# Shared experts' down products moved to the joining phase, with a chunked last batch and early first gathers

## The chip, the cores and the metric

One core of a Trainium2 chip runs the whole program. Its engines are TensorE (PE; PEld is its weight load), VectorE (DVE), ScalarE (ACT) and GpSimd (POOL); SyncE (SP) issues most of the DMAs, ACT and POOL issue some. They run their own instruction lists and meet by semaphores. The metric is the time of one execution on the device in microseconds (us).

## What is computed

A stack of four residual steps on 4 x 512 tokens of width 512. Each step is x = x + layernorm(f(layernorm(x))). The first f is a state-space layer, the second a mixture of experts, the third a gated delta-rule attention, the fourth an expert layer with routing by batch. The change touches the end of the first, the whole of the second, and the begin of the third. The second, cut to what matters:

```python
scores = softmax(x @ gate_weight.T)
topk_w, topk_idx = top_k(scores, 2)
gu = einsum('th,efh->tef', x, gate_up_weights)        # 8 experts, F = 352
act = silu(gu[..., :F]) * gu[..., F:]
y = einsum('tef,te,ehf->th', act, combine, down_weights)
sgu = x @ shared_gate_up.T                            # shared experts, 2 x 352
sact = silu(sgu[:, :Fs]) * sgu[:, Fs:]
y = y + sact @ shared_down.T
```

## The kernel before

Everything is float32 and runs in phases. A phase ends when all engines, SP too, are through with their lists, so also with the stores that SP waits for. A batch is 512 tokens (NB = 4 of them), handled as TPB = 4 chunks of 128 tokens on the partitions, or turned (features on the partitions) in XT, a tile of 4 batches x 4 x 512 that lasts through the phases.

**State space** (`phase_ssm`). Its last part norms the result y of each batch, adds it to x, norms the new x into yn, stores x and yn to HBM (x1 and xn), and PE turns yn into XT, ACT copying out of PSUM. For each of the last two batches DVE does it step by step for all four chunks: `y_mean`, `y_rstd` (the reciprocal root by 15 small DVE instructions), `y_apply`, `x_mean`, `x_rstd`, `x_apply`. PE turns the last batch at `turn(NB + 3)`.

**Shared experts and routing** (`phase_moe_shared`). For each batch PE makes five pairs of products g and u (`up`; the sixth pair, the one that carries the routing logits, is made for all batches first), ACT takes silu(g), DVE multiplies by u into `act`; then `downs(b)` makes 24 products of 128 x 512 into four PSUM banks, ACT copies them to `y` (`copies`), SP stores them to HBM (`y_shared`). Beside this DVE works out which slot each token takes, and POOL scatters the token numbers to HBM and reads them back (`rt.token`); SP loads the routed experts' gate and up weights.

**Routed experts** (`phase_moe_experts`). 40 tiles of 128 slots. SP first issues the loads of eight experts' down weights (`w_dn`, 768 KB each). POOL gathers a tile's rows from xn by token number (`gather`), two buffers deep; the first gather is its first work in the phase. PE turns the rows, makes g and u, turns the next tile's rows, and makes the down product of the tile before (`down`). In tile 0, which has no tile before it, PE waits at that place for all of `w_dn` (`dn_loaded`).

**Joining phase** (`phase_moe_out`). For each batch POOL gathers the two routed results of every token (`picked`, 8 gathers of 256 KB), SP loads y_shared and x1 of the batch, DVE sums them (`sums`), then DVE and ACT in turns do the two norms and the residual (`scale_y`, `residual`, `scale_x`), PE turns the result and ACT copies it to XT (`take_turned`). In between PE makes 12 units of the next layer's projections in three PSUM banks `pj` (`unit`), and ACT and DVE their convolution taps. After it comes the delta phase.

The order on each engine is the order of the code; there is no scheduler. The place on which PE waits in the routed phase:

```python
                if is_first(t):
                    e.wait_ge(dn_loaded, 16 * NE)
                else:
                    down(t - 1, 1 - par)
                e.wait_ge(act_done, t + 3)
```

## Time and profile before

| | us |
|---|---|
| median of 3 runs (lowest, highest) | 3064.32 (3063.19, 3068.24) |
| the profiled execution | 3064.84 |
| its span, first to last instruction | 3063.1 |
| mean granted TensorE clock | 0.961 |
| PE busy | 2827.2 (92%) |
| DVE busy | 1840.4 (60%) |
| ACT busy | 1203.1 (39%) |
| POOL busy | 612.7 (20%) |
| state space, until | 439.2 |
| shared experts and routing, until | 696.7 |
| routed experts, until | 1041.7 |
| joining phase, until | 1174.6 |

Times in a row are us from the span's start, unless marked ns. In brackets stands how long the engine was idle before, and what ended it: "<-DMA x" a landed transfer, "<-issue" nothing that the profile shows. A matmul of float32 is two passes on PE and counts as x2. The granted clock is a share of 2.4 GHz, so 0.50 is 1.2 GHz.

### The profile page before, as it was taken

How to read it: one execution, taken by the hardware profiler on the slowest of the kernel's cores; microseconds unless marked ns; L12 is line 12 of the kernel's file. 1: busy time of each engine (PE TensorE's matmuls, PEld its weight loads, DVE VectorE, ACT ScalarE, POOL GpSimd, SP SyncE). 2: the span in 40 equal slices, each digit the busy share in tenths (PEclk: the TensorE clock that was granted, in tenths of full speed). 3: DMA queues.
4: the chain of work that ended last, by engine and by line, in shares of the span. 5: the costliest groups of instructions: out<-in, count | busy, mean ns of one | idle time of the engine just before them, and what ended most of it. 6: DMA issues, size and time to landing. Idle time of an engine off the chain costs nothing. (4 is left out here: it accounts for less than half of the span.)

```text
span 3063.1 us, 37789 instructions
## 1 busy us (share of the span) xinstructions
PE 2827.2 (92%) x13038; PEld 1586.5 (52%) x13039; DVE 1840.4 (60%) x4673; ACT 1203.1 (39%) x2198; POOL 612.7 (20%) x669
## 2 busy tenths in 40 slices
PE   7999979997999587899999999999999999999787
PEld 3444434444565344555566655666556665554232
DVE  5767742000111275777877778777787777637676
ACT  4545511001212144345544455444554455422232
POOL 1111201301111312033123331233312333110000
PEclk9999989998999888999999999999999999999899
DMA  3100142003221452011100111001110011227213
GB/s 124 47 14 28 42 172 102 14 14 144 65 65 63 174 217 101 1 43 61 65 28 29 42 62 64 28 29 43 63 63 28 29 42 59 80 82 245 76 45 97
DMA packets 78134, 213.64 MB, mean 70 GB/s; under 512 B 12032, under 2 KB 12944, under 8 KB 69392
## 3 DMA queue, kind: packets, MB, share of 16 engines
q1 hardware_dynamic: 58336, 166.31, 15.0%
q0 software_dynamic: 9264, 28.36, 2.9%
q10 hardware_dynamic: 10368, 16.83, 1.5%
q8 instruction: 96, 1.57, 0.2%
q14 instruction: 70, 0.57, 0.1%
HBM read 154.68 MB, written 56.79 MB: 69 GB/s over the span
## 5 line engine op out<-in xcount | busy, mean ns | idle before, releaser
L2137 DVE SCALAR_TENSOR_TENSOR c_conv<-c_ps_pj,c_conv_t,c_conv 128x511 f32<-128x511 f32 (+2 forms) x495 | 368.0, 746 | 85.6 <-ACT c_conv L1975 73.9
L1759 PE MATMUL c_ps_pj<-c_w_g,c_xs 128*128 128x512 f32 x512 | 227.7, 592 | 0.0
L1668 POOL TENSOR_SCALAR c_gate<-c_gate 128x512 f32<-128x512 f32 x64 | 40.8, 637 | 932.6 <-ACT c_gate L1967 932.6
L1742 PE MATMUL c_ps_pj<-c_xs,c_w_v 128*128 128x512 f32 x480 | 225.8, 593 | 0.0
L1742 PE MATMUL c_ps_pj<-c_xs,c_w_k 128*128 128x512 f32 x480 | 218.0, 597 | 6.0 <-DMA c_xs<-xt_d 6.0
L1742 PE MATMUL c_ps_pj<-c_xs,c_w_q 128*128 128x512 f32 x360 | 195.3, 677 | 0.3
L1975 ACT ACTIVATE c_conv<-c_ps_pj,c_conv_t 128x512 f32<-128x512 f32 x165 | 127.9, 775 | 87.9 <-PE c_ps_pj L1742 85.8
L1098 DVE TENSOR_TENSOR x_act<-x_hs,x_ps_u 128x352 f32<-128x352 f32 x40 | 20.9, 521 | 228.0 <-ACT x_hs L1083 228.0
L2156 DVE TENSOR_TENSOR c_block_X<-c_block_X,c_block_t 128x126 f32<-128x126 f32 (+22 forms) x496 | 142.6, 288 | 17.0
L2152 DVE TENSOR_TENSOR c_block_t<-c_block_L,c_block_X 128x126 f32<-128x126 f32 (+22 forms) x496 | 139.4, 281 | 17.0
L1759 PEld LDWEIGHTS c_ps_pj<-c_w_g,c_xs 128*128 128x128 f32 x512 | 93.6, 190 | 100.0 <-issue 100.0
L880 DVE TENSOR_TENSOR b_act<-b_hs,b_ps_u 128x512 f32<-128x512 f32 (+1 forms) x24 | 16.5, 686 | 209.9 <-PE b_ps_u L802 209.9
L2027 ACT ACTIVATE c_err<-c_negL 32x128 f32<-32x128 f32 x256 | 78.6, 307 | 151.1 <-DVE c_negL L2221 146.4
L1742 PEld LDWEIGHTS c_ps_pj<-c_xs,c_w_k 128*128 128x128 f32 x480 | 87.3, 192 | 93.5 <-issue 87.2
L277 PE MATMUL a_ps_gt<-XT,a_w_gate 128*128 128x512 f32 x256 | 120.0, 613 | 6.5 <-ACT a_th L386 6.5
L1049 PE MATMUL x_ps_g<-b_w_gu,x_xT 128*128 x320 | 123.3, 467 | 1.6 <-issue 0.8
L245 POOL TENSOR_SCALAR a_skip<-a_xc,a_col_d 128x512 f32<-128x512 f32 x32 | 62.1, 1940 | 300.4 <-ACT a_xc L394 168.6
L1050 PE MATMUL x_ps_u<-b_w_gu,x_xT 128*128 x320 | 122.0, 463 | 0.0
L268 PE MATMUL a_ps_pj<-XT,a_w_in 128*128 128x512 f32 x256 | 119.1, 609 | 0.8 <-ACT XT L370 0.8
L294 PE MATMUL a_ps_yo<-a_w_out,a_th 128*128 128x512 f32 x256 | 115.7, 600 | 0.0
L1809 PE MATMUL c_ps_kk<-c_kT 128*128 128x128 f32 x512 | 101.5, 280 | 12.5 <-DVE XT L2223 7.0
L2086 ACT ACTIVATE c_err<-c_ps_z 128x512 f32<-128x512 f32 x64 | 38.2, 597 | 190.1 <-PE c_ps_z L1927 188.5
(499 smaller groups left out, 5907.2 us busy)
## 6 DMA issues: line engine op xcount, KB each, us to landing
c_G<-cum_d SPq DMA_DIRECT2D x16, 1024.0 KB, 4.7
c_xs<-xt_d SPq DMA_DIRECT2D x16, 1024.0 KB, 4.9
ot_d<-c_oT ACTq DMA_DIRECT2D x64, 256.0 KB, 2.0
b_w_gu<-in_w_gu SPq DMA_DIRECT2D x8, 1408.0 KB, 20.7
y_slots<-x_y SPq DMA_DIRECT2D x40, 256.0 KB, 2.0
a_x<-in_x SPq DMA_DIRECT2D x8, 1024.0 KB, 6.4
d_x<-x SPq DMA_DIRECT2D x32, 256.0 KB, 2.9
d_switch<-in_switch_w SPq DMA_DIRECT2D x4, 2048.0 KB, 15.3
```

Of the source, the lines that this page charges most:

```text
L268: mm = e.matmul(pj[c % 2][:, :], w_in[:, k, c * P:(c + 1) * P], XT[:, b, k, :], start=(k == 0), stop=(k == KD - 1))
L277: mm = e.matmul(gt[:, :], w_gate[:, k, c * P:(c + 1) * P], XT[:, b, k, :], start=(k == 0), stop=(k == KD - 1))
L294: mm = e.matmul(yo[t % 2][:, :], th[:, b % 2, c, t * P:(t + 1) * P], w_out[:, c, :], start=(c == 0), stop=(c == CT - 1))
L1049: e.matmul(g_ps[par][:, 0:FE], xT[par][:, k, :], w_gu[:, expert, k, 0:FE], start=(k == 0), stop=(k == KD - 1))
L1050: mm = e.matmul(u_ps[par][:, 0:FE], xT[par][:, k, :], w_gu[:, expert, k, FE:2 * FE], start=(k == 0), stop=(k == KD - 1))
L1742: mm = e.matmul(bank_of[xb][u][:, :], w["kqv"[u // HG]][:, k, (u % HG) * DH:(u % HG + 1) * DH], xs[xb][:, k, :], start=(k == 0), stop=(k = ...
L1759: mm = e.matmul(pj[(xb + i) % 2][:, :], xs[xb][:, k, i * P:(i + 1) * P], w["g"][:, k, :], start=(k == 0), stop=(k == KD - 1))
L1809: e.matmul(kk[:, h, :], chunk(kT, h, c), chunk(kT, h, c), start=True, stop=True)
L1975: e.activation(conv[:, u % 4, :], bank_of[buf][u][:, :], ACT.Identity, bias=conv_t[buf][:, m, h, TAPS:TAPS + 1], scale=conv_t[buf][:, m, h ...
L2137: e.scalar_tensor_tensor(oc, bank_of[buf][u][:, 0:SEQ - s], conv_t[buf][:, m, h, TAPS - 1 - s:TAPS - s], oc, ALU.mult, ALU.add).then_inc(c ...
L2152: e.tensor_tensor(t, block_L[:, i + 1:BB, i].unsqueeze(2).to_broadcast([P, n, k]), block_X[:, i, 0:k].unsqueeze(1).to_broadcast([P, n, k]) ...
L2156: e.tensor_tensor(below, below, t, ALU.add).then_inc(sub_step, 1)
```

## The change

1. **Chunks.** The last batch of the state-space phase is normed chunk by chunk: DVE makes mean and variance of one chunk, ACT the reciprocal root (logarithm, exponential with scale -0.5), DVE goes on with the next chunk's work meanwhile. Batch 2 keeps the old form.
2. **Downs kept.** Batches 2 and 3 (`KEPT`) have no down products, copies and stores in the shared phase. Their activations stay: five tiles of each in XT, which is free there, the sixth in the space of `s_gu0`, where DVE copies it. The shared down weights are loaded again in the routed phase, two DMAs of 768 KB behind the eight of `w_dn` on SP, into the last six tiles of XT. The joining phase makes the eight products (6 matmuls each): seven first of all on PE, the eighth after the first batch is turned. ACT copies each out of `pj` into one of four buffers and issues its store itself: five in front of its first norm, one each after `scale_y(0)`, `scale_x(0)` and `take_turned(0)`. The first unit waits for the last copy.
3. **Gathers.** The gathers of tiles 0 and 1 are issued by POOL at the end of the shared phase, right behind the token table's load. Its loop in the routed phase starts with tile 2 and waits for a copy of its own from two tiles earlier, not for the one just made.
4. **Wait.** The wait for `w_dn` moves from tile 0 into `down`, so to the first down product.

The core of the diff:

```diff
+GATED = len(FT) - 1
+UNGATED = [f for f in range(NSH * len(FT)) if f != GATED]
+KEPT = [NB - 2, NB - 1]
...
+            def root(v, c):
+                at = ve if v == 0 else rt
+                e.wait_ge(last_mean[v], c + 1)
+                e.activation(at[:, c:c + 1], mv[:, c, 1:2], ACT.Ln, bias=con["eps"][:, :]).then_inc(last_ln[v], 1)
+                e.wait_ge(last_ln[v], c + 1)
+                e.activation(rs[:, c:c + 1], at[:, c:c + 1], ACT.Exp, scale=-0.5).then_inc(last_rstd[v], 1)
             take_y(NB - 1, 0)
             take_y(NB - 1, 1)
             turn_tile(NB + 2, 0)
+            root(0, 0)
+            root(0, 1)
             take_y(NB - 1, 2)
             turn_tile(NB + 2, 1)
+            root(1, 0)
+            root(0, 2)
             turn_tile(NB + 2, 2)
+            root(1, 1)
             take_y(NB - 1, 3)
             turn_tile(NB + 2, 3)
...
+            root(0, 3)
+            root(1, 2)
+            turn_tile(NB + 3, 0)
+            turn_tile(NB + 3, 1)
+            root(1, 3)
+            turn_tile(NB + 3, 2)
+            turn_tile(NB + 3, 3)
...
-            for b in range(NB - 2, NB):
-                y_mean(b)
-                y_rstd(b)
-                y_apply(b)
-                x_mean(b)
-                x_rstd(b)
-                x_apply(b)
...
+            def last_means(v, c):
+                e.bn_stats(st_[:, c, :], (y, x)[v][:, c, :]).then_inc(last_stats[v], 1)
+                e.wait_ge(last_stats[v], c + 1)
+                e.bn_aggr(mv[:, c, :], st_[:, c, :]).then_inc(last_mean[v], 1)
+            def last_means_y(c):
+                e.wait_ge(y_free, b * TPB + c + 1)
+                last_means(0, c)
...
+            def last_add(c):
+                e.wait_ge(last_rstd[0], c + 1)
+                e.wait_ge(turn_ready, TPB * (NB + b - 1) + c + 1)
+                e.tensor_scalar(yn[:, c, :], y[:, c, :], mv[:, c, 0:1], rs[:, c:c + 1], ALU.subtract, ALU.mult).then_inc(last_y, 1)
+                if c == 0:
+                    e.wait_ge(x_loaded, 16 * (NB + b + 1))
+                e.wait_ge(last_y, c + 1)
+                e.tensor_tensor(x[:, c, :], x[:, c, :], yn[:, c, :], ALU.add).then_inc(x_new, 1)
+                e.wait_ge(x_new, b * TPB + c + 1)
+                last_means(1, c)
...
+            def last_scale(c):
+                e.wait_ge(last_rstd[1], c + 1)
+                e.tensor_scalar(yn[:, c, :], x[:, c, :], mv[:, c, 0:1], rs[:, c:c + 1], ALU.subtract, ALU.mult).then_inc(x_normed, 1)
+            last_means_y(0)
+            last_means_y(1)
+            e.wait_ge(xn_stored, 16 * b)
+            last_add(0)
+            last_means_y(2)
+            last_add(1)
+            last_scale(0)
+            last_add(2)
+            last_scale(1)
+            last_means_y(3)
+            last_scale(2)
+            last_add(3)
+            last_scale(3)
...
+class KeptShared:
+    def __init__(self, XT, s_gu0):
+        tiles = XT[:, :, :, :].rearrange("p b k s -> p (b k) s")
+        self.w_dn = tiles[:, NB * KD - NSH * len(FT):, :].rearrange("p (i f) d -> p i f d", i=NSH)
+        gated = s_gu0[:, :, :].rearrange("p k f -> p (k f)")[:, 0:len(KEPT) * SEQ]
+        self.gated = gated.rearrange("p (b s) -> p b s", b=len(KEPT))
+        self.acts = tiles
+    def act(self, b, f):
+        j = KEPT.index(b)
+        if f == GATED:
+            return self.gated[:, j, :]
+        return self.acts[:, j * len(UNGATED) + UNGATED.index(f), :]
...
-            with e.Fori(0, NB) as b:
+            for b in range(NB - len(KEPT)):
                 for c in range(TPB):
                     e.wait_ge(y_copied, b * TPB + c + TPB + 1)
-                    stand(e, pr.waits_passed)
-                    e.dma_start(io["y_shared"][b].rearrange("(c p) d -> c p d", p=P)[c], y[c % 2][:, :]).then_inc(y_stored[c % 2], 16)
+                    e.dma_start(rows(io["y_shared"], b)[:, c, :], y[c % 2][:, :]).then_inc(y_stored[c % 2], 16)
...
+            e.wait_ge(token_loaded, 16)
+            for i in range(2):
+                e.tensor_copy(rows_in.one_token[i][:, :], rt.token[:, i:i + 1]).then_inc(first_copied, 1)
+            for i in range(2):
+                e.wait_ge(first_copied, i + 1)
+                e.indirect_dma_start(rows_in.x[i][:, :], None, io["xn"].rearrange("b s d -> (b s) d"),
+                                     bass.IndirectOffsetOnAxis(rows_in.one_token[i][:, :], 0)).then_inc(rows_in.loaded[i], 16)
...
-                downs(b)
+                if b not in KEPT:
+                    downs(b)
...
+                if b not in KEPT:
+                    copies(b)
...
+                    dst = kept.act(b, f) if b in KEPT and f != GATED else act[:, slot(b, f), :]
+                    e.tensor_tensor(dst[0:width, :], hs[s % 2][0:width, :], u_ps[s % 2][0:width, :], ALU.mult).then_inc(act_done, 1)
...
+                if b == NB - 1:
+                    acts(of_batch(b, 0, NF - 2))
+                    for k in KEPT:
+                        e.tensor_copy(kept.act(k, GATED)[0:GW, :], act[0:GW, slot(k, GATED), :]).then_inc(gated_kept, 1)
+                    acts(of_batch(b, NF - 2))
+                else:
+                    acts(of_batch(b))
...
+            for i in range(NSH):
+                e.dma_start(kept.w_dn[:, i], io["w_dn"][NE + i]).then_inc(kept_loaded, 16)
...
+                e.wait_ge(copied, t - 1)
...
-            tiles(e, gather)
+            with e.Fori(0, NS // 2 - 1) as p:
+                gather(p * 2 + 2, 0, p + 1)
+                gather(p * 2 + 3, 1, p + 1)
...
+                e.wait_ge(dn_loaded, 16 * NE)
...
-                if is_first(t):
-                    e.wait_ge(dn_loaded, 16 * NE)
-                else:
+                if not is_first(t):
...
+                    for stored in down_stored:
+                        e.wait_ge(stored, 16 * (b + 1))
...
+            def down(i):
+                b, c = downs[i]
+                if i >= PJ:
+                    e.wait_ge(down_copied, i - PJ + 1)
+                order = [GATED] + UNGATED
+                for f in order:
+                    width = FT[f % len(FT)][1]
+                    mm = e.matmul(pj[i % PJ][:, :], kept.act(b, f)[0:width, c * P:(c + 1) * P], kept.w_dn[0:width, f // len(FT), f % len(FT), :],
+                                  start=(f == order[0]), stop=(f == order[-1]))
+                mm.then_inc(down_ready, 1)
...
+                elif u == 0:
+                    e.wait_ge(down_copied, len(downs))
...
+            for i in range(len(downs) - 1):
+                down(i)
...
+                if b == 0:
+                    down(len(downs) - 1)
...
+            def take_down(i):
+                b, c = downs[i]
+                e.wait_ge(down_ready, i + 1)
+                if i >= STAGES:
+                    e.wait_ge(down_stored[i % STAGES], 16 * (i // STAGES))
+                e.activation(first.conv[:, i % STAGES, :], pj[i % PJ][:, :], ACT.Copy).then_inc(down_copied, 1)
+                e.wait_ge(down_copied, i + 1)
+                e.dma_start(rows(io["y_shared"], b)[:, c, :], first.conv[:, i % STAGES, :]).then_inc(down_stored[i % STAGES], 16)
...
+            for i in range(5):
+                take_down(i)
             scale_y(0)
+            take_down(5)
             scale_x(0)
+            take_down(6)
             take_turned(0)
+            take_down(7)
```

On DVE at the end of the state-space phase, before: the last batch from its y scale on; a_st, a_mv are statistics, a_ve, a_rt, a_rs the root's tiles.

```order
L512 TENSOR_SCALAR a_yn<-a_y,a_mv,a_rs 128x512 x4
L517 TENSOR_TENSOR a_x<-a_x,a_yn 128x512 x4
L480 BN_STATS a_st<-a_x 128x6 x4
L483 BN_AGGR a_mv<-a_st 128x2 x4
L114 TENSOR_SCALAR a_ve<-a_mv 128x4
L116 TENSOR_SCALAR a_rt<-a_ve 128x4
```

And now, from chunk 1's y scale on:

```order
L633 TENSOR_SCALAR a_yn<-a_y,a_mv,a_rs 128x512
L637 TENSOR_TENSOR a_x<-a_x,a_yn 128x512
L622 BN_STATS a_st<-a_x 128x6
L624 BN_AGGR a_mv<-a_st 128x2
L643 TENSOR_SCALAR a_yn<-a_x,a_mv,a_rs 128x512
L633 TENSOR_SCALAR a_yn<-a_y,a_mv,a_rs 128x512
L637 TENSOR_TENSOR a_x<-a_x,a_yn 128x512
L622 BN_STATS a_st<-a_x 128x6
L624 BN_AGGR a_mv<-a_st 128x2
L643 TENSOR_SCALAR a_yn<-a_x,a_mv,a_rs 128x512
L622 BN_STATS a_st<-a_y 128x6
```

Each step of four is now one of a chunk, and the small steps of the root are gone from DVE.

On PE at the last batch of the shared phase, the end of it and the first turned tile of the routed phase (b_ps_y are the down products), before:

```order
L802 MATMUL b_ps_u<-XT,b_s_gu 128x512 x4
L802 MATMUL b_ps_g<-XT,b_s_gu 96x512 x4
L802 MATMUL b_ps_u<-XT,b_s_gu 96x512 x4
L808 MATMUL b_ps_y<-b_s_dn,b_act 128x512 x24
L677 UNCONDITIONAL_BRANCH
L1027 UNCONDITIONAL_BRANCH
L1032 MATMUL x_ps_xt<-ident,x_x 128x128 x4
```

And now:

```order
L895 MATMUL b_ps_g<-XT,b_s_gu 128x512 x4
L895 MATMUL b_ps_u<-XT,b_s_gu 128x512 x4
L895 MATMUL b_ps_g<-XT,b_s_gu 96x512 x4
L895 MATMUL b_ps_u<-XT,b_s_gu 96x512 x4
L764 UNCONDITIONAL_BRANCH
L1133 UNCONDITIONAL_BRANCH
L1138 MATMUL x_ps_xt<-ident,x_x 128x128 x4
```

The 24 down products between the last product and the next phase are gone; those of batch 2, one batch up, too.

On ACT in the joining phase, from the first norm of batch 0 to that of batch 1 (c_conv is the buffer of a kept product, o_ps_pj its bank), before:

```order
L1280 ACTIVATE o_y_ln<-o_y_mv,eps 128x4
L1282 ACTIVATE o_y_rs<-o_y_ln 128x4
L1286 ACTIVATE o_yn<-o_y,o_y_nb,o_y_rs 128x512 x4
L1280 ACTIVATE o_x_ln<-o_x_mv,eps 128x4
L1282 ACTIVATE o_x_rs<-o_x_ln 128x4
L1286 ACTIVATE o_xn<-o_x,o_x_nb,o_x_rs 128x512 x4
L1301 ACTIVATE XT<-o_ps_tp 128x4x128 x4
L1280 ACTIVATE o_y_ln<-o_y_mv,eps 128x4
L1282 ACTIVATE o_y_rs<-o_y_ln 128x4
```

And now, behind five pairs of copy and store:

```order
L1409 ACTIVATE o_y_ln<-o_y_mv,eps 128x4
L1411 ACTIVATE o_y_rs<-o_y_ln 128x4
L1415 ACTIVATE o_yn<-o_y,o_y_nb,o_y_rs 128x512 x4
L1449 ACTIVATE c_conv<-o_ps_pj 128x512
L1451 DMA y_shared<-c_conv 128x512
L1409 ACTIVATE o_x_ln<-o_x_mv,eps 128x4
L1411 ACTIVATE o_x_rs<-o_x_ln 128x4
L1415 ACTIVATE o_xn<-o_x,o_x_nb,o_x_rs 128x512 x4
L1449 ACTIVATE c_conv<-o_ps_pj 128x512
L1451 DMA y_shared<-c_conv 128x512
L1430 ACTIVATE XT<-o_ps_tp 128x4x128 x4
L1449 ACTIVATE c_conv<-o_ps_pj 128x512
```

Three more pairs of copy and store stand between the norms and the turned tiles; the last pair stands in front of batch 1's first norm.

## Rows read from the trace of the kernel before

**Rows 1.** Busy time per stretch: us, then each engine's busy us; clock, DMA share, GB/s

```profile
439.20:696.70 257.50, 252.91 (x596) 108.33 (x596) 27.86 (x69) 30.35 (x48) 39.73 (x93) 0.98 0.18 73
696.70:1041.70 345.00, 328.22 (x1160) 196.21 (x1160) 45.57 (x120) 66.57 (x121) 46.40 (x80) 0.97 0.23 79
1041.70:1174.60 132.90, 79.86 (x298) 47.85 (x298) 84.75 (x167) 59.21 (x100) 32.91 (x32) 0.75 0.58 215
```

**Rows 2.** Timeline, PE and SP, end of state space; landing of a_x, of xn

```profile
431.63 1.11 PE L256 MATMUL a_ps_tp<-ident,a_yn 128*128 128x128 f32 x4 [14.84 <-DVE a_yn L490]
...
439.34 6.50 PE L802 MATMUL b_ps_g<-XT,s_gu 128*96 128x512 f32 x8 [1.00 <-POOLq L752]
...
404.61 0.45 SPq L211 DMA_DIRECT2D a_x<-in_x  x1
...
432.97 0.36 SPq L215 DMA_DIRECT2D xn<-a_yn  x1
...
DMA to landing us min/median/max: 7.5/7.5/7.5
...
DMA to landing us min/median/max: 4.2/4.6/5.1
```

**Rows 3.** Groups by shape, DVE, 300 to 440 (busy, mean ns); timeline, ACT, joining phase

```profile
L517 DVE TENSOR_TENSOR a_x<-a_x,a_yn 128x512 f32<-128x512 f32 x12 | 7.5, 682 | 0.0
L480 DVE BATCH_NORM_STATS2 a_st<-a_x 128x6 f32<-128x512 f32 x12 | 7.4, 676 | 0.0
...
L490 DVE TENSOR_SCALAR a_yn<-a_x,a_mv,a_rs 128x512 f32<-128x512 f32 x12 | 5.7, 541 | 0.1
...
L483 DVE BATCH_NORM_AGGREGATE a_mv<-a_st 128x2 f32<-128x6 f32 x24 | 2.2, 151 | 0.0
...
1064.70 0.30 ACT L1280 ACTIVATE o_y_ln<-o_y_mv,eps 128x4 f32<-128x4 f32 x1 [21.64 <-DVE o_y_mv L1364]
1065.03 0.21 ACT L1282 ACTIVATE o_y_rs<-o_y_ln 128x4 f32<-128x4 f32 x1
```

**Rows 4.** Timeline, PE, DVE and ACT, shared experts and the edge after them

```profile
668.04 3.60 PE L802 MATMUL b_ps_u<-XT,b_s_gu 128*96 128x512 f32 x8
671.47 20.78 PE L808 MATMUL b_ps_y<-b_s_dn,b_act 96*128 96x512 f32 x48
...
616.72 0.68 DVE L880 TENSOR_TENSOR b_act<-b_hs,b_ps_u 96x512 f32<-96x512 f32 x1 [6.18 <-PE b_ps_u L802]
...
696.73 1.28 ACT L1070 ACT_TABLE_LOAD   x1 [2.67 <-PEq L677]
```

**Rows 5.** Timeline, PE, begin of the routed experts

```profile
705.91 1.09 PE L1032 MATMUL x_ps_xt<-ident,x_x 128*128 128x128 f32 x4 [13.66 <-DMA x_x<-xn,x_one_token]
...
717.00 0.55 PE L1060 MATMUL x_ps_at<-ident,x_act 128*128 128x128 f32 x3 [2.06 <-DMA x_w_dn<-in_w_dn]
...
725.19 2.74 PE L1040 MATMUL x_ps_y<-x_w_dn,x_actT 128*128 x6
...
733.27 2.74 PE L1040 MATMUL x_ps_y<-x_w_dn,x_actT 128*128 x6
```

**Rows 6.** Timeline, DVE, PE and ACT, joining phase; one stretch of it

```profile
1060.47 0.75 DVE L1379 SCALAR_TENSOR_TENSOR o_y<-o_picked,route_weight,o_shared 128x512 f32<-128x512 f32 x1 [1.05 <-DMA o_picked<-y_slots,route_slot]
...
1073.57 1.97 PE L1228 MATMUL o_ps_tp<-ident,o_xn 128*128 128x128 f32 x8 [35.01 <-issue]
...
1078.97 12.72 PE L1249 MATMUL o_ps_pj<-XT,c_w_k 128*128 128x512 f32 x24 [0.78 <-ACT XT L1301]
...
1081.20 0.30 ACT L1280 ACTIVATE o_y_ln<-o_y_mv,eps 128x4 f32<-128x4 f32 x1 [2.38 <-issue]
...
1357.49 0.60 ACT L1985 ACTIVATE c_oT<-c_ps_d 128x512 f32<-128x512 f32 x1 [2.15 <-DMA ot_d<-c_oT]
1358.11 0.33 ACTq L1987 DMA_DIRECT2D ot_d<-c_oT  x1
...
1078.00:1082.00 4.00, 3.22 (x5) 1.51 (x5) 3.26 (x10) 1.10 (x3) 2.67 (x3) 0.50 1.04 412
```

60 lines of the change are left out of this document (38 added, 22 removed).

## The prediction

> **What bounds the kernel now.** I read the stages first (busy time per stretch) [rows 2], then the edges between them in order of time, since the change touches edges. TensorE (PE) is busy 253 of 257.5 us in the stretch of the shared experts, and 328 of 345 in that of the routed ones; in the joining phase only 80 of 132.9, at a mean clock of 0.75 [rows 1]. So work of PE taken from the second stretch and put into idle time of the fourth is gained as a whole, unless what it delays there is on the joining phase's own path. That path is VectorE (DVE) and ScalarE (ACT) in turns; PE first works at 1073.57 [rows 6]. At the other edges PE waits: 14.84 us for the layer norms of the last batch of the state-space phase [rows 2], 13.66 us for the first gathered rows, and again until the down weights have landed at 717.00 [rows 5]. All sums go against the profiled execution, 3064.84 us for a span of 3063.1 (1.7 us around it); the median of three runs, 3064.32, is 0.5 us less.
>
> **A. Last state-space batch by chunks: -8.0 us.** Now all four chunks pass each step together, with two reciprocal roots of 15 small DVE instructions; PE gets its first chunk at 431.63, and starts the next phase at 439.34 [rows 2]. In the new order a chunk costs DVE, in a chain: scale 0.54, add 0.72 and statistics 0.72 with their 0.04 of waiting, and 0.19 for the aggregate, 2.17 us, and later 0.5 for the second scale [rows 3]. ACT's logarithm and exponential are 0.30 and 0.21 us [rows 3]; 0.55 with the way between. The start is not set by DVE: the add needs the batch's x, issued at 404.61 and landed 7.5 us later, at 412.1 [rows 2]. From there, in DVE's written order: add, statistics and aggregate of chunk 0 until 413.8; statistics of y chunk 2 414.7; chunk 1 416.9; scale 0 417.4; chunk 2 419.5; scale 1 420.0; statistics of y chunk 3 420.9. Now DVE waits for two roots that stand in a row on ACT (y 3, then x 2, 1.1 us): scale 2 422.6; chunk 3 424.8; root 0.55; scale 3 426.0. PE and ACT need some 2 us more for the last turned tile (428.1), but SyncE's queue (SP) holds the end: the store of xn, issued at 426.0, landed after 4.2 us at the quickest in the rows [rows 2], and the x1 store just ahead of it takes some of the bandwidth: 430.9. PE starts near 431.3 against 439.34: 8.0 us. The bounds: 10.5 if the store lands as PE ends, 6 if each of some twelve hand-overs costs 0.15 more. New behind ACT's waits: the copy of y chunk 3 stands behind the root of x chunk 1, so it comes 1.2 us later, and DVE takes it only at 420.0: nothing. The first matmuls of the next phase are slow in both cases (6.50 us for eight passes [rows 2] against 20.78 / 48 = 0.43 each in the dense row [rows 4]).
>
> **B. Down products of batches 2 and 3 leave the shared phase: -44.7 us.** Each batch is 24 matmuls in 48 passes, 20.78 us, of which 0.17 lies over what stands beside it (668.04 + 3.60 is 671.64, not 671.47): 20.6 net [rows 4]. Batch 2's lies between products without a gap: 20.6. Batch 3's is the tail: it starts at 671.47, and the next phase at 696.73, after PE's 20.6, the last copies on ACT and their stores [rows 4]. In the new kernel the phase ends with DVE's last product, 0.68 us long, behind PE's last pass at 671.64 [rows 4]: 672.3, and 672.6 with the barrier, where 696.73 was. That is 24.1 us, and 20.6 + 24.1 = 44.7. Added are two DVE copies of 96x512 between products that DVE awaits for 6 us at a time, two token copies and two gathers on POOL at about 595 in a phase that now ends at 652, and a store loop that SP executes half as often: all hidden. If the gathers' cover were gone, they would cost their 7-9 us again.
>
> **C. First gathers early, wait for the down weights later: -5.8 us.** Count from the phase's start T (696.7 before). The down weights are loaded from T on and let PE go at 717.00, T + 20.3 [rows 5]. That doesn't move: it is DMA. What PE does before it does: tile 0's rows lie there already, ACT's table load ends at T + 1.3, its copy at T + 1.9, and both products of tile 0 and 1 and three turns are done by about T + 13.5. Then the moved wait, now in front of the first down product, holds PE until T + 20.3. Before, that product starts at 725.19, T + 28.5 [rows 5]. Gross 8.2 us. PE idles some 6.8 us there, and starts again at the low clock: a start of this kind costs 2.4 us by 24 passes in 12.72 us where 10.3 are due [rows 6], and 3.1 by the eight in 6.50 [rows 2]; I take 2.4, since short rows mix in. Net 5.8; the bounds are 8.2 (the clock holds) and 3.5 (the two kept loads of 0.77 MB each, behind the eight on SP's queue, run beside them and not after them, which would be a quarter of 18 us more, with half of it felt). In the loop the wait is passed at once, beside a 64-pass stretch of PE: nothing. The gather of tile t still goes out when tile t - 2's rows are turned, with a tile's time to land, 733.27 - 725.19 = 8.08 us [rows 5]. Its wait on its own copies is for older ones now, two tiles back; the copy of 0.2 us is long done.
>
> **D. The downs in the joining phase: +9.7 us.** From here all is in before's times. PE starts at 1041.9, cold: chunk i is ready at 1041.9 + 2.4 + 5.15 (i + 1), with 12 passes of 0.43 [rows 4]. ACT has five copies, with a store issued after each (0.60 + 0.35 us, as such pairs take elsewhere [rows 6]), in front of its first root. The fifth chunk comes at 1070.1, so that root starts at 1071.1 and not at 1064.70 [rows 3]: +6.4 us, felt whole, because DVE and ACT work in turns from here. The sixth copy (ready 1075.2) fits behind the first scale. PE ends the seventh at 1080.4, when the rows that it has to turn are ready anyway (1073.57 + 6.4). The seventh copy and store stand ahead of the turned tiles on ACT (its first is taken at 1073.57 + 1.97 = 1075.54 [rows 6], which with 6.4 is 1081.9, and becomes 1083.0), and PE's third and fourth turn wait for these: PE turns until 84.7, then the eighth down, 5.15: 1089.9, copy and store 1090.9. Behind them stands ACT's root of batch 1, which was at 1081.20 [rows 6] and would be at 1087.6: another +3.3. The first unit waits for the last copy, starts at 1090.5, and its result is there before ACT asks, at 1094.6, after that batch's scale. Units 0 to 3 and the gate products then bring PE to the second turn at 1107.8, 9.3 us later than now: no further loss. Bounds: 7.3 if PE starts warm; 13 if the pause of 2.4 us before the third turn makes the eighth down cold, and up to 20 if the stores collide with the gathers as in the rival below.
>
> **DMA in the joining phase.** In the rows the 16 engines are full there (share 1.04 at 412 GB/s between 1078 and 1082), and the last pair of batch 0's picked rows releases DVE at 1060.47 [rows 6]. By then ACT has issued two or three stores of 0.26 MB, 0.8 MB or 2 us of all bandwidth. The root waits for the fifth down until 1071.1, and so 6.4 us of delay cost nothing. The Trainium skill, "DMA: Bandwidth & Descriptors", section on queues, rings and completion order, has each DMA engine go round robin between the queues with work. By it a third queue would take a third of the time while it has work, and a picked row would lose at most about 3 us: the sum stays, and the chance of the collision below goes down.
>
> **The sum.** -8.0 - 44.7 - 5.8 + 9.7 = -48.8; 3064.84 - 48.8 = 3016.0, and 3015.5 as a median, or 1.6% faster.
>
> **Rivals.**
> *The clock holds* across the short waits (C 8.2, D 7.3) and the store is off the path of A (up to 10.5): -53.6 to -56, 3008 to 3011. For it: at T + 13.5 PE has been dense. Against: eight passes in 6.50 us after the last turned tiles of the state-space phase, with 1 us of pause [rows 2]. 0.17.
> *The joining phase takes more*: eighth down cold, its store issue and copies later: D 13 to 17, 3019 to 3023. For it: there the clock is 0.50 even between 1078 and 1082, with PE at work [rows 6]. 0.17.
> *Collision*: the stores and the last downs also push the picked rows of batches 1 and 2 or the unit products behind, D 20 and more, 3026 to 3032. Against: batch 1's picked rows were never waited for. 0.05.
> *Slower than before*: PE falls to the low clock at the moved wait and stays there, since the tiles leave it pauses. A tile of 8.08 us would cost as much again; from the seventh such tile on (48.8 / 8.08 = 6.0) the gain is gone, and all 40 would cost 320. Against: the stretch runs at 0.97 now though it starts cold [rows 1]. 0.02.
>
> **How the numbers follow.** The forecast itself, 3011 to 3019, has 0.59. The range goes from 3007 to 3026 and leaves out the collision, the slower case and a little of each tail. A difference under 0.2%, 6 us, can hardly be told from no change in this kernel: faster 0.97, same 0.01, slower 0.02.
>
> **What would show it.** PE's first shared product near 431; the first routed turn near 652 - 8 = 644, warm; PE idle about 7 us in front of the first routed down, and 36 to 38 us of downs at the joining phase's start; ACT's first root 6 us later against the phase's start than now, the second one 10. The joining phase should be 9.7 us longer, the delta phase the same length. The forecast is wrong if that first root comes at its old time, or if the phase of the shared experts still ends with a store.

## The result and the profile after

The changed kernel takes **3016.82 us** (median of 4 runs, 3015.14 to 3020.22) where the kernel before takes 3063.99 us (4 runs beside it, 3063.19 to 3068.24): a ratio of 0.9847, 95% interval 0.9835 to 0.9859. The forecast of 3015.5 us was right to 1.3 us. Its profiled execution has a span of 3016.3 us, 46.8 us less than the 3063.1 of before.

The sum is made by stages. I take as edges the first thing that the next stage issues on SyncE (SP); for the end of state space, the time from the store of the last batch but one (the last `xn<-a_yn` with the load of `a_x` right behind it) to the next stage's first load; for the joining phase, the time to the store of `cum_d`.

| stretch | before, us | after, us | difference | forecast |
|---|---|---|---|---|
| end of state space (A) | 35.08 | 26.33 | -8.75 | -8.0 |
| shared experts (B) | 257.48 | 212.21 | -45.27 | -44.7 |
| routed experts (C) | 345.04 | 339.24 | -5.80 | -5.8 |
| joining phase (D) | 127.94 | 140.29 | +12.35 | +9.7 |
| sum of these | | | -47.47 | -48.8 |
| code ahead of them, unchanged | 404.16 | 401.41 | -2.75 | 0 |
| code behind them, unchanged | 1893.40 | 1896.82 | +3.42 | 0 |

The last two rows are no effect of the change: over the twelve kernels below the stretch behind is 1893.1 to 1898.2 us long and the one ahead 401.1 to 404.2, with no relation to the edits.

Busy time per stretch of the changed kernel (us, then each engine's busy us; clock, DMA share, GB/s), which answers to [rows 1]:

```profile
427.80:639.90 212.10, 211.10 (x500) 90.00 (x500) 28.53 (x71) 25.54 (x40) 41.99 (x97) 0.99 0.21 82
639.90:979.30 339.40, 326.82 (x1161) 195.06 (x1161) 45.64 (x121) 66.64 (x122) 44.11 (x76) 0.99 0.24 84
979.30:1120.00 140.70, 121.20 (x394) 65.31 (x394) 82.45 (x164) 59.73 (x102) 31.62 (x32) 0.88 0.58 217
```

PE had 253 us of work in 257.5 us of shared experts; it now has 211 in 212. The 42 us that left there stand in the joining phase, where PE is busy for 121 us and not 80, while the phase grew by 12. Its mean clock there rose from 0.75 to 0.88.

**End of state space.** Timelines of DVE, PE and SP, answering to [rows 2]:

```profile
409.43 0.69 DVE L637 TENSOR_TENSOR a_x<-a_x,a_yn 128x512 f32<-128x512 f32 x1 [2.44 <-DMA a_x<-in_x]
...
422.08 0.55 DVE L643 TENSOR_SCALAR a_yn<-a_x,a_mv,a_rs 128x512 f32<-128x512 f32 x1 [0.60 <-ACT a_rs L470]
...
422.66 0.36 SPq L220 DMA_DIRECT2D xn<-a_yn  x1
427.74 0.35 SPq L819 DMA_DIRECT2D b_s_gu<-in_w_gu  x1
...
427.85 5.93 PE L895 MATMUL b_ps_g<-XT,s_gu 128*96 128x512 f32 x8 [3.62 <-POOLq L838]
```

DVE's first add waits for the load of x (issued 401.87, so 7.5 us); its last scale comes 12.65 us later, where the forecast had 13.4; the store of `xn`, landed 4.63 us after its issue, then holds PE for 3.62 us after the turned tiles are done. That is the forecast's chain, with 0.75 us less in it.

**Edge to the routed experts and their begin.** DVE, PE and POOL, answering to [rows 4, 5]:

```profile
638.99 0.68 DVE L976 TENSOR_TENSOR XT<-b_hs,b_ps_u 96x512 f32<-96x512 f32 x1 [5.51 <-PE b_ps_u L895]
...
640.14 0.63 PE L1138 MATMUL x_ps_xt<-ident,x_x 128*128 128x128 f32 x4 [1.19 <-PEq L764]
641.99 0.85 PE L1156 MATMUL x_ps_g<-b_w_gu,x_xT 128*128 x2 [1.22 <-ACT x_xT L1179]
...
660.42 4.87 PE L1147 MATMUL x_ps_y<-x_w_dn,x_actT 128*128 x6 [5.53 <-DMA x_w_dn<-in_w_dn]
...
670.63 2.74 PE L1147 MATMUL x_ps_y<-x_w_dn,x_actT 128*128 x6
...
587.37 1.01 POOL L867 DMA_INDIRECT x_x<-xn,x_one_token  x1 [0.44 <-POOL x_one_token L864]
```

The shared experts end with DVE's product and no store. The first gathers went out at 587.37 and 588.68; PE turns the first tile 0.2 us after the stage's start (before: 9.2) and is warm: the turn takes 0.63 us and not 1.09. It then stands for the down weights until 660.42, 20.47 us after the start. The first six down matmuls take 4.87 us where six take 2.74 in the next tile: 2.1 us for a cold start, where I had taken 2.4.

**Joining phase.** PE and ACT, answering to [rows 3, 6]; the phase starts at 979.19:

```profile
981.08 6.61 PE L1340 MATMUL o_ps_pj<-XT 128*128 128x512 f32 x10
987.52 1.02 PE L1340 MATMUL o_ps_pj<-XT,s_gu 96*128 96x512 f32 x2
988.38 4.46 PE L1340 MATMUL o_ps_pj<-XT 128*128 128x512 f32 x10
...
1018.44 1.13 PE L1351 MATMUL o_ps_tp<-ident,o_xn 128*128 128x128 f32 x8
1021.89 1.12 PE L1351 MATMUL o_ps_tp<-ident,o_xn 128*128 128x128 f32 x8 [2.33 <-ACT XT L1430]
1022.85 1.82 PE L1340 MATMUL o_ps_pj<-XT,s_gu 96*128 96x512 f32 x2
1024.47 5.40 PE L1340 MATMUL o_ps_pj<-XT 128*128 128x512 f32 x10
...
1009.34 0.30 ACT L1409 ACTIVATE o_y_ln<-o_y_mv,eps 128x4 f32<-128x4 f32 x1 [0.41 <-ACT c_conv L1449]
...
1029.90 0.60 ACT L1449 ACTIVATE c_conv<-o_ps_pj 128x512 f32<-128x512 f32 x1 [6.25 <-PE o_ps_pj L1340]
...
1030.96 0.30 ACT L1409 ACTIVATE o_y_ln<-o_y_mv,eps 128x4 f32<-128x4 f32 x1 [0.46 <-ACT c_conv L1449]
```

The first root of ACT is 30.15 us after the start (before 22.94), the second 51.77 (before 39.44): +7.2 and +12.3, against a forecast of +6.4 and +9.7. The first down takes 8.3 us (979.24 to 987.52) and not 5.15, the eighth 7.0 (1022.85 to 1029.87): after a wait of 2.33 us between the turns PE is slow again. The granted clock of the stretch of the first down, then of the eighth, is 0.63 and 0.76:

```profile
979.24:987.52 8.28, 8.28 (x12) 3.47 (x13) 0.28 (x1) 1.25 (x1) 5.79 (x7) 0.63 0.83 307
1022.85:1029.87 7.02, 7.01 (x14) 2.67 (x12) 2.90 (x9) 0.80 (x2) 4.99 (x6) 0.76 0.85 272
```

From the second root to the end the two kernels run alike: third and fourth root are 65.75 and 91.19 us after the start before, 78.07 and 103.52 after, 12.3 late all along.

### The profile page after: what moved, and what is told of

Read it like the earlier page. It is cut to its first block and busy times, and to the rows that moved or that the text cites. A ratio compares the mean times of both kernels' runs of the same rounds, so it can differ in the third digit from the quotient of the medians.

```text
span 3016.3 us, 37740 instructions
## 1 busy us (share of the span) xinstructions
PE 2824.9 (94%) x13038; PEld 1584.4 (53%) x13039; DVE 1837.2 (61%) x4645; ACT 1206.1 (40%) x2214; POOL 611.9 (20%) x669
## 5 line engine op out<-in xcount | busy, mean ns | idle before, releaser
L1147 PE MATMUL x_ps_y<-x_w_dn,x_actT 128*128 (+1 forms) x240 | 111.9, 603 | 6.4 <-DMA x_w_dn<-in_w_dn 5.5
## 6 DMA issues: line engine op xcount, KB each, us to landing
b_w_gu<-in_w_gu SPq DMA_DIRECT2D x8, 1408.0 KB, 20.8
```

The source lines that it names most:

```text
L1147: mm = e.matmul(y_ps[par][:, :], actT[par][0:width, f, :], w_dn[0:width, expert, f, :], start=(f == 0), stop=(f == NF - 1))
```

## The experiments

Twelve kernels were run in groups 2 to 5, one of them the changed kernel once more (group 1 is its own first measurement); kernels of one group ran beside the same runs of the kernel before, whose medians were 3062.3 to 3066.5 us. The table gives each kernel's time, its ratio to before, the stretches defined above from its profile, and when ACT's first and second root come, counted from the joining phase's start. Medians of different groups are better compared by their ratios. The group matters for one thing more, told under e8.

| kernel | group | median us | ratio, 95% interval | state-space end | shared | routed | joining | roots 1, 2 |
|---|---|---|---|---|---|---|---|---|
| before | | | | 35.08 | 257.48 | 345.04 | 127.94 | 22.94, 39.44 |
| after | 1 | 3016.82 | 0.9847, 0.9835-0.9859 | 26.33 | 212.21 | 339.24 | 140.29 | 30.15, 51.77 |
| e1_chunks | 2 | 3056.10 | 0.9977, 0.9967-0.9987 | 26.33 | 257.31 | 344.72 | 128.18 | 23.28, 39.78 |
| e2_downs | 2 | 3030.25 | 0.9890, 0.9875-0.9905 | 35.09 | 212.78 | 347.30 | 139.81 | 29.82, 51.43 |
| e3_gathers | 2 | 3064.05 | 1.0005, 0.9996-1.0014 | 36.25 | 257.55 | 344.53 | 128.22 | 23.10, 39.60 |
| e4_wait | 2 | 3063.30 | 0.9997, 0.9988-1.0006 | 36.30 | 257.50 | 342.20 | 127.22 | 22.08, 38.58 |
| after_again | 3 | 3022.66 | 0.9874, 0.9857-0.9891 | 26.31 | 211.99 | 339.34 | 142.85 | 31.55, 54.46 |
| e5_eight_row | 3 | 3017.84 | 0.9854, 0.9838-0.9869 | 26.32 | 212.14 | 339.16 | 142.30 | 35.74, 52.25 |
| e6_three_first | 3 | 3019.63 | 0.9861, 0.9845-0.9877 | 26.32 | 212.05 | 339.16 | 140.12 | 23.80, 51.48 |
| e7_spread | 3 | 3013.82 | 0.9842, 0.9828-0.9857 | 27.96 | 212.97 | 339.60 | 136.34 | 24.26, 45.39 |
| e9_spread_stages | 4 | 3006.17 | 0.9806, 0.9793-0.9819 | 27.79 | 211.31 | 338.85 | 128.92 | 24.02, 40.52 |
| e10_thin | 4 | 3011.05 | 0.9819, 0.9805-0.9833 | 27.93 | 212.99 | 339.60 | 130.31 | 23.75, 40.25 |
| e11_last_only | 4 | 3027.08 | 0.9880, 0.9865-0.9895 | 26.23 | 232.80 | 338.64 | 130.39 | 24.02, 40.52 |
| e8_stages | 5 | 3019.94 | 0.9860, 0.9843-0.9876 | 26.38 | 212.56 | 339.34 | 144.09 | 33.45, 55.69 |

Two differences at the end of the state-space phase belong to no edit there. In e7, e9 and e10 the store of `xn` lands 6.24 us after its issue, in the other kernels with chunks after 4.63 to 4.65: 1.6 us more before the next phase. In e3 and e4 that stretch is 1.2 us longer than before. Neither was followed.

My theory at this point: four edits with four prices that add, and a joining phase that is late because ACT has five copies and PE eight downs ahead of the two first roots. Rivals: the stages lean on each other, so that the parts don't add; and within the joining phase, that ACT's copies, or PE's downs, or PE's total work set the delay.

### Each part alone

**e1_chunks**, the kernel before with the chunked end of the state-space phase; all its lines are in that phase:

```
-            for b in range(NB - 2, NB):
-                y_mean(b)
-                y_rstd(b)
...
+            last_means_y(0)
+            last_means_y(1)
+            e.wait_ge(xn_stored, 16 * b)
+            last_add(0)
+            last_means_y(2)
+            last_add(1)
+            last_scale(0)
...
```

> The kernel before with one edit: the last state-space batch runs its tail by chunks. The part theory (each edit is worth what its stage lost in the changed kernel, and the parts add): the end of state space, 35.08 us between the last batch's first store and the next stage in the kernel before, was 26.33 us in the changed kernel, so this kernel alone is 8 to 9 us shorter than before, about 3055.5 us. Rival, the stages lean on each other: the shared experts' first product waits for weights or turned tokens that are not there 8 us earlier when nothing else is changed; then the end of state space is still about 26 us long, but the shared experts are longer by the same, and the time is 3060 to 3064 us.

Measured: the end of state space is 26.33 us, as in the changed kernel, and the shared experts are not longer for it (257.31). Stage and time agree: -8.75 in the profile, a ratio of 0.9977, or -7 us with an interval from 4 to 10. The edit is worth its stage.

**e2_downs**, the kernel before with the downs of the last two batches kept and run in the joining phase, and nothing else:

```
+KEPT = [NB - 2, NB - 1]
...
-                downs(b)
+                if b not in KEPT:
+                    downs(b)
...
+            for i in range(len(downs) - 1):
+                down(i)
```

> The kernel before with one edit: the shared experts' down products of the two last batches are kept and run at the joining phase's start. Part theory: the shared experts lose 45 us (44.7 forecast, 45.27 read in the changed kernel) and the joining phase gains 12.3 us (127.94 us before, 140.29 us in the changed kernel): net -33 us, about 3031 us. Forecast as it stood: -44.7 and +9.7, net -35.0 us, about 3029 us. Rival, the joining phase's 12.3 us are owed to the stages ahead of it and not to the downs (what the first gathers or the chunks left behind): then it is 128 to 133 us long here and the time is about 3023 us.

Measured: 3030.25 us, -34 us by the ratio; shared experts -44.70, joining phase +11.87. So those 12 us belong to the downs and to nothing ahead of them. The routed experts, whose edits are not in it, took 2.3 us more than before: their down weights landed 21.2 us after the start and not 20.3, and in the second tile the pairs of matmuls stayed slow (1.38 us) for 6 us where before they were back at 0.76 after 3.4. Why, was not followed.

**e3_gathers** and **e4_wait** split part C. The one issues the two first gathers ahead of the last shared products, the other moves the wait.

In e3, POOL's code of the shared experts:

```
+            for i in range(2):
+                e.wait_ge(first_copied, i + 1)
+                e.indirect_dma_start(rows_in.x[i][:, :], None, io["xn"].rearrange("b s d -> (b s) d"),
+                                     bass.IndirectOffsetOnAxis(rows_in.one_token[i][:, :], 0)).then_inc(rows_in.loaded[i], 16)
```

> The kernel before with one edit: the two first gathers of the routed experts are issued ahead of the last shared products; the wait for the down weights stays where it was, at the first tile's end. The theory of two locks: TensorE starts its first turn under 1 us after the stage's start (9 us before), but then stands before the first down until the same weights land, 20 us after the start, as in the kernel before, and every later row is where it was: the time is that of the kernel before within 1 us, about 3064 us. Rival, the gathers were the only lock: the routed experts are 5 to 8 us shorter and the time is 3056 to 3059 us.

In e4, PE's code of the routed experts (first the down product, then the tile):

```
+                e.wait_ge(dn_loaded, 16 * NE)
...
-                if is_first(t):
-                    e.wait_ge(dn_loaded, 16 * NE)
-                else:
+                if not is_first(t):
                     down(t - 1, 1 - par)
```

> The kernel before with one edit: the wait for the routed down weights stands ahead of the first down product and no longer at the first tile's end, with the gathers late as before. The theory of two locks: TensorE starts 9 us after the stage's start as before, has the first and second tile's gate and up products done some 25 us after it, by when the down weights (20.5 us) are there, and so runs through: the first down starts about 25 us after the start where before it was 28.5, so that 2.5 to 3.5 us go, about 3061 us. Rivals: the gathers alone hold the stage, 0 us (3064); or the wait alone held it, and all 5.8 us of the changed kernel's gain come here (3058).

The timeline of PE at the begin of the routed experts, e3 first (stage start 694.97), then e4 (695.09):

```profile
695.16 1.09 PE L1049 MATMUL x_ps_xt<-ident,x_x 128*128 128x128 f32 x4 [4.75 <-PEq L686]
...
714.30 0.90 PE L1077 MATMUL x_ps_at<-ident,x_act 128*128 128x128 f32 x3 [9.08 <-DMA x_w_dn<-in_w_dn]
...
722.91 2.74 PE L1057 MATMUL x_ps_y<-x_w_dn,x_actT 128*128 x6
```

```profile
704.22 1.09 PE L1032 MATMUL x_ps_xt<-ident,x_x 128*128 128x128 f32 x4 [13.62 <-DMA x_x<-xn,x_one_token]
...
714.02 0.55 PE L1059 MATMUL x_ps_at<-ident,x_act 128*128 128x128 f32 x3 [0.74 <-DVE x_act L1097]
...
720.65 2.74 PE L1041 MATMUL x_ps_y<-x_w_dn,x_actT 128*128 x6
```

In e3 PE starts 9 us earlier and hands them back: it stands 9.08 us before the down weights, and the first down comes 27.9 us after the start (before 28.5). In e4 it starts as late as before, but is never held again: the first down comes 25.6 us after the start. The stretch is 0.51 us shorter in e3, 2.84 in e4, and 5.80 with both. Two locks hung on one door: the early gathers are worth about nothing alone and 3 us beside the moved wait. Both kernels' times are those of before within their intervals: e4's 2.84 us stand on the profile alone, and 1.2 us of them are lost there at the end of the state-space phase.

### What sets the joining phase's length

**after_again**, **e5_eight_row** and **e6_three_first** ran together. e5 puts the eighth down into PE's row (and its copy ahead of the turned tiles on ACT):

```
-            for i in range(len(downs) - 1):
+            for i in range(len(downs)):
                 down(i)
...
-                if b == 0:
-                    down(len(downs) - 1)
```

e6 moves ACT's copies and leaves PE alone:

```
-            for i in range(5):
+            for i in range(3):
                 take_down(i)
             scale_y(0)
-            take_down(5)
+            take_down(3)
+            take_down(4)
             scale_x(0)
+            take_down(5)
```

> The changed kernel once more, on the same chip as the three that vary it: 3015 to 3020 us, and the joining phase 140 us long as in its first profile. It is the base from which the other three of this call are read.

> The changed kernel with the eighth down product pulled into the row of the seven ahead of the joining phase's first turn; ScalarE copies it before it copies the first turned tiles. Theory of the cold eighth down: where it stands in the changed kernel it cost about 7 us (an idle of 2.33 us ahead and 1.82 and 5.40 us at the low clock) against the 5.15 us of one in a row; in the row it costs 5.15 us ahead of the first root and nothing between: the first root comes 0 to 5 us later and the second one 3 to 4 us earlier; the time is 2 to 4 us under the changed kernel. Rival: what counts is the work that stands ahead of the second root in total, so that one down costs the same in either place: within 1 us of the changed kernel. Other side: the first root waits 5 us more and nothing is won back: 3 to 5 us over it.

> The changed kernel with ScalarE's copies in another order: three of the kept down products are copied ahead of the first root, two after the first scaling and one after the scaling of the other branch (five stood ahead of the root). Theory that I forecast by (the first root comes late since five copies stand ahead of it): the first root comes 5 to 6 us earlier, and the time is about 6 us under the changed kernel. Rival, TensorE's row of seven downs sets the delay, and the copies ahead of the root only fill ScalarE's wait: the root comes 0 to 2 us earlier, and the time is within 1.5 us of the changed kernel.

ACT and PE in e6, whose joining phase starts at 981.61:

```profile
1005.41 0.30 ACT L1409 ACTIVATE o_y_ln<-o_y_mv,eps 128x4 f32<-128x4 f32 x1 [3.96 <-DVE o_y_mv L1509]
...
1015.04 0.60 ACT L1449 ACTIVATE c_conv<-o_ps_pj 128x512 f32<-128x512 f32 x1 [5.87 <-remote]
...
1033.09 0.30 ACT L1409 ACTIVATE o_y_ln<-o_y_mv,eps 128x4 f32<-128x4 f32 x1 [0.46 <-ACT c_conv L1449]
...
1016.65 4.46 PE L1340 MATMUL o_ps_pj<-XT 128*128 128x512 f32 x10
1020.95 1.04 PE L1351 MATMUL o_ps_tp<-ident,o_xn 128*128 128x128 f32 x8
```

**The first root moved 6.35 us forward against the first profile of the changed kernel (23.80 for 30.15), and the second root 0.29 (51.48 for 51.77).** So the delay of the first root, which I had called felt whole, is hardly felt at all. What holds the second root is PE: its row of seven downs runs without a gap until 39.3 us after the phase's start, in both kernels, where the turns came at 31.8 before; then come the wait between the turns, the eighth down and its copy, which ACT makes ahead of that root. Against the repeat in its own group the two roots are 7.75 and 2.98 us earlier: there the turns wait 1.17 us more, for ACT's rows, by a stand of ACT that is told below. e6 has such a stand too, of 5.87 us: ACT has the first rows scaled 37.6 us after the phase's start, only 1.3 us earlier than in the first profile. They lie ready for 1.7 us before PE is free, so that the reading holds, but e6 did not take the full 6.4 us off ACT's path. The time, 3019.63 us, is 3 us under the repeat, with intervals that overlap, and not 6 us under.

In e5 the first root is 5.6 us later than in the first profile of the changed kernel, all of it by the same stand, and the second 0.5 us (52.25 for 51.77; 54.46 in the repeat). By the length of the phase the eighth down costs about the same in the row as behind the turns. The times, 3017.84 and 3022.66 us, have overlapping intervals, and the joining phases are 0.55 us apart: I read no gain in it.

**e7_spread** takes both readings together: PE gets six downs, the turn, a down, three unit products, a down, the second turn; ACT copies three, then two, then one at a time:

```
-            for i in range(len(downs) - 1):
+            for i in range(6):
                 down(i)
...
+            turn(0)
+            down(6)
+            unit(0)
+            unit(1)
+            unit(2)
+            down(7)
+            turn(1)
```

> The changed kernel with the eight kept downs spread thinner: six at the start, one after the first turn, one after the third unit, and ScalarE's copies spread alike (three ahead of the first root). Theory: the joining phase's start has TensorE idle in several places, and its 12.3 us of growth come from work that stands in a row ahead of the two first roots; spread, each copy and each down lies in an idle stretch, and the phase is 2 to 6 us longer than in the kernel before and not 12.3: 6 to 10 us under the changed kernel, about 3008 us. Rival: the phase was bound by TensorE's work in total at its low clock, and the eight downs cost about 1.5 us each wherever they stand: within 2 us of the changed kernel, or over it where a down comes cold.

Measured: the median is 8.8 us under the repeat in its group, within the theory's 6 to 10, and the joining phase 6.5 us shorter (136.34 for 142.85). But the time is 3013.82 and not 3008 us, and the phase is still 8.4 us longer than before and not 2 to 6. The rest begins in ACT's timeline, before its fourth copy (the phase starts at 984.72):

```profile
1009.80 2.93 ACT L1427 ACTIVATE o_yn<-o_y,o_y_nb,o_y_rs 128x512 f32<-128x512 f32 x4 [0.29 <-issue]
1018.73 0.60 ACT L1461 ACTIVATE c_conv<-o_ps_pj 128x512 f32<-128x512 f32 x1 [6.00 <-remote]
...
1020.79 0.30 ACT L1421 ACTIVATE o_x_ln<-o_x_mv,eps 128x4 f32<-128x4 f32 x1 [0.40 <-ACT c_conv L1461]
...
1022.48 1.97 PE L1354 MATMUL o_ps_tp<-ident,o_xn 128*128 128x128 f32 x8 [3.30 <-ACT o_xn L1427]
```

ACT stood 6.00 us, until 34.0 us after the start, before a copy whose down had ended on PE at 1008.87. The root of the other branch came behind it, and the turn 3.30 us after PE was free for it. Behind that wait PE is cold: its granted clock is 0.65 in the 14 us from the first turn, where e9 below, which has no stand, has 1.00 (1022.40 to 1036.40 and 1015.60 to 1029.60). The second root is 6.0 us later than before, the third 8.5. The same stand is in e6 (until 33.4), and in the repeat of the changed kernel and in e5 before the fifth copy (until 30.6 and 34.7). In the first profile of the changed kernel it is not there: hence the 2.6 us between the two.

### A second buffer set, and the stand of ACT

**e9_spread_stages** is e7 with eight buffers for the copies and not four used twice; **e10_thin** also puts one unit product ahead of the seventh down and gives the two last downs PSUM banks of their own. The edit of the copies, cut to its core:

```
-    STAGES = 4
+    STAGES = 8
...
-                if i >= STAGES:
-                    e.wait_ge(down_stored[i % STAGES], 16 * (i // STAGES))
-                e.activation(first.conv[:, i % STAGES, :], pj[bank(i)][:, :], ACT.Copy).then_inc(down_copied, 1)
+                e.activation(staged(i), pj[bank(i)][:, :], ACT.Copy).then_inc(down_copied, 1)
...
```

and in e10, PE's order:

```
             turn(0)
+            unit(0)
             down(6)
-            unit(0)
             unit(1)
```

> The thinly spread kernel of the call before (joining phase 136.3 us) with one edit: the eight kept down products are copied into eight buffers and not into four used twice, so that no copy waits for a store. In that kernel ScalarE stood 6.0 us before its fourth copy, and its second root's pair came 4.7 us after the statistics were there; in a repeat of the changed kernel the fifth copy was 1.6 us late, with a wait on the store of the first copy in front of it. Theory, stores that land late hold ScalarE: the stand of 6.0 us is gone, the joining phase is 131 to 133 us long, 3 to 5 us less. Rival, the stand has another cause (the fourth copy itself had no store to wait for in the program): it stays 5 to 6 us, and the joining phase 135 to 137 us.

> A candidate to beat both kernels: as the one before, with eight buffers, and the two last downs in PSUM banks of their own (unused until the end of the phase), so that no unit product waits for their copies: six downs, first turn, first unit product, down, two unit products, down, second turn. Theory (what costs in the joining phase is what stands ahead of each root, not the work in total): the second root, 39.4 us after the phase's start before and 45.4 in the spread kernel, comes at 40 to 41, the third at 66 to 68, and the phase is 129 to 131 us long, 10 us under the changed kernel: about 3008 us. Rival, TensorE's total work at its low clock binds: 134 us or more, and a time within 4 us of the changed kernel's.

ACT and PE of e9, whose joining phase starts at 981.80:

```profile
1005.82 0.30 ACT L1421 ACTIVATE o_y_ln<-o_y_mv,eps 128x4 f32<-128x4 f32 x1 [4.84 <-DVE o_y_mv L1525]
...
1009.47 0.57 ACT L1463 ACTIVATE c_conv<-o_ps_pj 128x512 f32<-128x512 f32 x1
...
1022.32 0.30 ACT L1421 ACTIVATE o_y_ln<-o_y_mv,eps 128x4 f32<-128x4 f32 x1 [2.20 <-DVE o_y_mv L1525]
...
1015.64 1.04 PE L1354 MATMUL o_ps_tp<-ident,o_xn 128*128 128x128 f32 x8
1018.37 1.12 PE L1354 MATMUL o_ps_tp<-ident,o_xn 128*128 128x128 f32 x8 [1.69 <-ACT XT L1442]
1019.32 1.02 PE L1343 MATMUL o_ps_pj<-XT,s_gu 96*128 96x512 f32 x2
1020.18 4.46 PE L1343 MATMUL o_ps_pj<-XT 128*128 128x512 f32 x10
```

**e9 beats both kernels**: 3006.17 us, ratio 0.9806 (0.9793 to 0.9819), whose interval lies clear below that of the changed kernel (0.9835 to 0.9859). Its joining phase is 128.92 us long, 1 us over the kernel before, with all eight downs in it, and shorter than both sides of its expectation had it; ACT's roots wait for DVE again and not for a copy. The seventh down, behind a wait of 1.69 us, is warm (1.02 and 4.46 us, at a granted clock of 1.00 from 1019.32 to 1024.64). The joining phase of e9, then of e10, as a stretch (columns as in [rows 1]), with PE busy for 118 us of it at a mean clock of 0.90:

```profile
981.80:1110.72 128.92, 117.54 (x394) 65.27 (x394) 82.43 (x164) 59.29 (x102) 32.37 (x32) 0.90 0.62 237
...
981.64:1111.95 130.31, 117.95 (x394) 63.87 (x394) 82.56 (x164) 59.23 (x102) 32.12 (x32) 0.90 0.61 235
```

e10 does in the profile what its expectation said (second root at 40.25, third at 66.56, 130.31 us), but its time is 3011.05 us and not 3008 (3005.0 to 3013.6), and it gives nothing over e9: in both the first two roots wait for DVE, and PE's order between them moves the second by 0.27 us. The rival that PE's total work binds has fallen: the eight downs, 41.2 us of it at 5.15 each, cost 1 us of time where they stand well.

But was it the buffers that made e9 shorter than e7? **e8_stages** is the changed kernel with eight buffers and its own order:

> The changed kernel with eight buffers for the copies of the kept downs and nothing else: the fourth of four cases (order of the changed kernel or spread, four buffers or eight). Spread with eight buffers has a joining phase of 128.9 us, spread with four 136.3, the changed kernel 140.3 and 142.9 in two profiles. Theory, in the changed kernel's order TensorE's row of seven downs and the eighth one set the second root, so that buffers alone give nothing but the 2.6 us by which those two profiles differ: joining phase 140 us, second root 51 to 52 us after the start, time 3014 to 3020 us. Rival, the store waits are what made the changed kernel's joining phase long, and the order matters little: 131 to 135 us and 3008 to 3012 us.

ACT in e8 (phase start 979.38):

```profile
1003.49 0.60 ACT L1451 ACTIVATE c_conv<-o_ps_pj 128x512 f32<-128x512 f32 x1 [4.56 <-issue]
1004.12 0.33 ACTq L1453 DMA_DIRECT2D y_shared<-c_conv  x1
1011.83 0.60 ACT L1451 ACTIVATE c_vT<-o_ps_pj 128x512 f32<-128x512 f32 x1 [7.74 <-issue]
...
1012.83 0.30 ACT L1409 ACTIVATE o_y_ln<-o_y_mv,eps 128x4 f32<-128x4 f32 x1 [0.40 <-issue]
```

The stand is there again, 7.74 us where 4.56 are due, until 32.5 us after the start, though no copy in this kernel waits for a store; the joining phase is 144.09 us, outside of both expectations, and 1.2 us longer than that of the repeat, which has the same order, four buffers and the stand too. The time, 3019.94 us, is that of the theory. **So the theory of the late stores has fallen, and e9's gain over e7 is not shown to be that of the buffers.** The stand goes by group: it is in all five profiles of groups 3 and 5, and in none of the five of groups 1, 2 and 4 that have kept downs, whatever the order and the number of buffers. It always lies between 27 and 35 us after the phase's start. It does not go by the chip: groups 2 and 5 ran on the same one.

What ACT waits for is the count `down_ready`, which PE raises with the last matmul of each down; every copy waits for it. The traces keep the time at which a count rises. In us from the phase's start:

| profile | down | its last matmul ends | count rises | copy starts |
|---|---|---|---|---|
| after | fifth | 29.10 | 29.12 | 29.14 |
| after_again | fifth | 28.95 | 30.53 | 30.56 |
| e5_eight_row | fifth | 29.12 | 34.72 | 34.74 |
| e6_three_first | fourth | 23.92 | 33.41 | 33.43 |
| e7_spread | fourth | 24.15 | 33.99 | 34.01 |
| e8_stages | fifth | 29.23 | not recorded | 32.45 |

In the profiles without a stand every rise comes 0.01 to 0.02 us behind the matmul's end. In those with it, the rise that ACT needs comes 1.6 to 9.8 us late, and the copy starts 0.02 to 0.03 us behind it; the sixth down's count is still 0.3 to 0.9 us late, and from 39 us on those recorded are on time. So the copy did have something to wait for: **the stand is a count of PE that rose late.** The DMA engines are as full in the one as in the other, as a stretch of e8, then one of the first profile of the changed kernel show:

```profile
1003.38:1009.38 6.00, 6.00 (x16) 2.64 (x15) 0.38 (x5) 0.60 (x1) 4.48 (x6) 1.00 1.04 400
...
1003.19:1009.19 6.00, 6.00 (x15) 2.65 (x14) 1.05 (x6) 1.18 (x2) 4.69 (x5) 1.00 1.04 398
```

In the profiles that have the stand, most rises of counts are not recorded in just that time: 126 to 152 are in the first 35 us of the phase, where the five other profiles with kept downs have 555 to 567. The landings of ACT's first stores are among the missing; in the others the first four land 6.8 to 10.2 us after their issue. Records are missing in the profile of the kernel before as well (344), whose roots come as in e1 and e3, so that this alone does not make a delay that shows. Why the counts rise late, and whether it has to do with the recording, is open.

What this leaves of the comparisons: The 7.4 us by which e9's phase is shorter than e7's go with the stand and the low clock behind it. e7 and the repeat of the changed kernel share the stand, and the spread order is 6.5 us better in the profile (136.34 for 142.85) and 9 us in the medians, though their intervals touch. e9 and the changed kernel's first profile are both without it, and the spread order is 11.4 us better (128.92 for 140.29) and 10.7 us in the medians, 12.6 by the ratios. The first pair differs in the order alone, and in the old order eight buffers gave nothing (144.09 for 142.85, both with the stand). Both say that the order was the gain; whether the eight buffers have a share in e9's was not settled, since no run has the spread order, four buffers and no stand.

**e11_last_only** keeps the last batch's four downs alone:

```
-KEPT = [NB - 2, NB - 1]
+KEPT = [NB - 1]
```

> The changed kernel with only the last batch's four downs kept for the joining phase (three copies ahead of the first root). Theory, four downs in a row end 24 us after the phase's start, before TensorE is wanted at 31.8, and so cost nothing: joining phase 128 to 129 us (127.94 before, 140.3 with eight), shared experts 20.6 us longer than in the changed kernel, 233 us; the time is 8 to 9 us over the changed kernel, 3025 to 3028 us. Rival, part of the 12.3 us is a price of the first downs (cold start, copies and stores beside the gathers): 131 us or more, and 3028 to 3033 us.

Measured: roots at 24.02 and 40.52, exactly those of e9 with eight; shared experts 232.80, +20.6 over the changed kernel as computed; joining phase 130.39, between the 128 to 129 of the theory and the 131 of the rival; 3027.08 us. Four downs are over before PE is wanted. The first root of e9, e10 and e11 comes 23.8 to 24.0 us after the start, against 22.1 to 23.3 in the four kernels without kept downs: about 1 us is all that kept downs cost on that path if they stand well. The 1.5 us that e10 and e11 have over e9 come behind the fourth root, as 1.6 us do in e5 against the repeat, where I didn't follow them.

## Why the prediction was right

**A, -8.0; measured -8.75.** The chain is the one that was worked out: load of x, four chunks through DVE, two waits for roots of ACT, then the store of `xn`. Behind the add, hand-overs cost 0.75 us less than supposed. The rival in which the store is off the path did not come: PE stood 3.62 us for it.

**B, -44.7; measured -45.27** (-44.70 in e2). Twice 20.6 us of dense PE work and the tail of copies and stores: both bounds were rows of the trace, and both held. The copies, gathers and stores that were put at nothing cost nothing that shows.

**C, -5.8; measured -5.80.** The first turn came at 640.14, warm, and the wait for the down weights took 5.53 us ahead of the first down, where I had some 7: the two tiles' products took a little longer than supposed, which costs nothing in front of a wait. Weights at 20.47 us after the start (20.3), restart 2.1 us (2.4), later rows in step. That the two edits have to come together (0.51 and 2.84 alone) the sum had not said, though its working holds it: the gathers only bring work ahead of a lock that the other edit moves.

**D, +9.7; measured +12.35.** The steps that failed are two, one of size and one of cause.

- *Size.* "PE starts at 1041.9, cold" had 2.4 us for that start, and it took 3.1 (8.3 for 5.15); the eighth down was put at 5.15 us, warm, and took 7.0 from start to end where one in the row takes 5.3, cold after the 2.33 us between the turns. These two make some 2.5 of the 2.65 us that D came out over the forecast. The forecast had named this as the bound of 13 ("makes the eighth down cold") and gave the rival 0.17; the value came out nearer to that end than to the one I took. The trace of before had it: behind the wait of 2.06 us that ends at 717.00 [rows 5], and another of 0.81, PE's next pair of matmuls takes 1.54 us and not 0.76, and I had read a wait of the same length in the new order and put it at nothing.

```profile
718.35 1.54 PE L1049 MATMUL x_ps_g<-b_w_gu,x_xT 128*128 x2 [0.81 <-issue]
```

- *Cause.* "+6.4 us, felt whole, because DVE and ACT work in turns from here" is wrong. e6 took those 6.4 us off the first root and the second hardly moved. There are two paths to the second root: DVE and ACT in turns, and PE's row of seven downs, the turns, the eighth down, its copy. I had followed the second one too ("PE ends the seventh at 1080.4, when the rows that it has to turn are ready anyway") and found the two level at the turns. So they are: in the first profile ACT has the first rows scaled 39.0 us after the phase's start, and PE turns at 39.3. But of two level paths neither alone carries a delay, and the text gave it to one. In e6 the first path is shorter, by 1.3 us at the turns since its stand gave most of the gain back, and PE's row alone has the turns 7.5 us late. The number came out near since the paths were level, not since the one named carried it.

Of the marks in "What would show it": first shared product 427.85 (forecast 431, of which 2.75 us are the unchanged code ahead), first routed turn 640.14, warm (644 less that drift and the 0.75 and 0.6 us of A and B), the row of seven downs 39.4 us (36 to 38: the start again), ACT's first root 7.2 us late (6), its second 12.3 (10), the joining phase 12.35 longer (9.7). The collision with the picked rows didn't come: the last of batch 0's picked rows lands 19.5 to 20.8 us after the phase's start beside the stores (after, e2, e9, e10, e11) and 17.8 to 19.0 without them (e1, e3, e4), with DMA engines that are full. Where the first root waits for DVE and not for a copy, it is about 1 us later than without the stores. By the Trainium skill ("DMA: Bandwidth & Descriptors", section on queues, rings and completion order), each engine goes round robin between the queues with work; the trace agrees in so far as neither side was shut out, the stores landing in 6.8 to 10.2 us and the picked rows losing 1 to 2 us, but the turns themselves are not to be seen in it.

The deviations of A, B and D (-0.75, -0.57, +2.65) and the drift of the unchanged code (-2.75 and +3.42) happen to leave 2.0 us of the span, and 1.3 us of the median: that the forecast is so near is luck, since D alone was 2.65 us off. A repeat on another occasion gave 3022.66, with the same A, B and C, and D at 14.9, 2.6 us more by the stand: within the range too, where the case lay that I had given 0.17, though only in part by its cause: the eighth down is cold in both profiles, and the stand was in no forecast.

## What to carry to other kernels

Work that is moved into an engine's idle time costs what it holds up at the next hand-over and not what it lasts: here eight down products cost 12 us of the joining phase with seven in a row, and 1 us when six stood ahead of the turn and the others between later waits. Where two paths meet at a point and your sum puts both at the same time, say so and price each alone: shortening the one you named may give nothing. And where two waits guard the same stretch, neither edit shows its worth alone; try them together before either is thrown away.

## What was not expected of the hardware

- A count that PE raises at the end of a product rose 1.6 to 9.8 us late (0.01 to 0.02 us otherwise) and held ACT for 1.6 to 6 us, 27 to 35 us after the start of the joining phase, in four of ten profiles of kernels with kept downs; in a fifth (e8) ACT stands alike, and the rise is not recorded. In the same stretch of the five most rises are missing from the trace. It went with the group of the run. Its cause is open.
- PE restarts cost 2.1 us (six matmuls in 4.87 for 2.74), 3.1 us (first down, 8.3 for 5.15) and 1.7 us (eighth down, 7.0 for 5.3, after a wait of only 2.33); in e6, after a wait of 2.04, the eighth down is slow too (1.60 and 5.62 us); in e9, after a wait of 1.69 us with no other just ahead of it, the same kind of down was warm. The granted clock was 0.50 from 1022.93 to 1026.35 in the changed kernel, and stayed at 1.00 in e9.
- The same store of `xn` took 6.24 us to land in three kernels (e7, e9, e10) and 4.63 to 4.65 in the others with the same code around it. Not followed.
- Unchanged code of some 1900 us differs by up to 5 us between profiles (1893.1 to 1898.2): differences of a few us are better read from the stretch than from the total.
